# Exponentials of the third to seventh pair one slot later, and another order of the scatters of the first two pairs

## The reference, cut to what matters

```python
z = relu(einsum('bsh,bhk->bsk', x, Wd[ids]) + bd[ids])
y = x + einsum('bsk,bkh->bsh', z, Wu[ids]) + bu[ids]
h = (y - mean(y)) * rsqrt(var(y) + 1e-5) * g[ids] + b[ids]      # 256 wide
p = softmax(h @ gate_w + gate_b)                                # 8 experts
v, i = top_k(p, 2);  v = v / (sum(v) + 1e-9)
mlp = lambda h, e: gelu(h @ w1[e] + b1[e]) @ w2[e] + b2[e]      # 256 -> 1024 -> 256
out = x + h + mlp(h, shared) + sum(v[k] * mlp(h, i[k]) for k in (0, 1))
```

## Time and profile before

| | us |
|---|---|
| median of 3 runs | 625.84 |
| lowest and highest | 624.57, 626.19 |
| the profiled execution's own time | 622.08 |
| its span, first to last instruction | 620.2 |
| TensorE busy in the span | 594.8 (96%) |
| VectorE, ScalarE, GpSimd busy | 501.6, 385.4, 413.3 |
| TensorE's mean granted clock | 0.997 of full speed |

### The profile page before, as it was taken

One profiled execution on the slowest core, in us unless ns is written; L12 is line 12 of the kernel. 1 busy time (PEld: TensorE's weight loads), 2 busy tenths in 40 slices (PEclk: granted clock), 3 DMA queues, 4 the chain that ended last, 5 costly groups with the idle time before them and its releaser, 6 DMA issues.

```text
span 620.2 us, 16942 instructions
## 1 busy us (share of the span) xinstructions
PE 594.8 (96%) x5119; PEld 483.3 (78%) x5119; DVE 501.6 (81%) x1212; ACT 385.4 (62%) x660; POOL 413.3 (67%) x326
## 2 busy tenths in 40 slices
PE   7889979999999999999999999999999999999994
PEld 3556646667566678788888888888888899999883
DVE  4999848879977966898989898989897587887862
ACT  2686928758776845767676767676755455555541
POOL 4564587989885611477868686858697567666682
PEclk9999999999999999999999999999999999999998
DMA  8985656575244945667657656665644335343212
GB/s 285 322 220 150 159 161 183 161 235 115 78 138 153 328 114 171 144 113 149 116 127 133 147 127 127 132 136 128 94 53 72 60 61 66 58 67 64 44 21 32
DMA packets 116740, 81.31 MB, mean 131 GB/s; under 512 B 71090, under 2 KB 106162, under 8 KB 116658
## 3 DMA queue, kind: packets, MB, share of 16 engines
q1 hardware_dynamic: 100802, 60.64, 39.7%
q0 software_dynamic: 13296, 16.92, 15.2%
q10 hardware_dynamic: 2560, 2.69, 1.4%
HBM read 43.21 MB, written 24.42 MB: 109 GB/s over the span
## 4 chain that ended last, share of the span: by engine, by line
PE 68%; DVE 8%; POOL 8%; issue 8%; ACT 4%; DMA 2%; SPq 0%; POOLq 0%; ACTq 0%; DVEq 0%
PE Y L1527 30%; PE H L1501 29%; PE Y L1419 5%; POOL xs_rows L534 3%; PE H L1404 3%; POOL wreg L502 2%; POOL wreg L512 2%; DMA wreg<-in_vecs 1%; ACT hf L685 1%; DVE hl L1160 1%; POOL wreg L516 1%; ACT L685 1%; DVE wreg L808 1%; ACT wreg L623 1%; DVE wreg L949 1%
## 5 line engine op out<-in xcount | busy, mean ns | idle before, releaser
L755 ACT ACTIVATE hf<-H,prme 128x256 f32<-128x256 f32 (+1 forms) x312 | 149.2, 544 | 95.9 <-issue 80.5
L1501 PE MATMUL H<-xT,wreg 128*128 128x256 f16 (+1 forms) x1872 | 194.4, 263 | 0.2
L1527 PE MATMUL Y<-wreg,hh 128*128 x1136 | 188.3, 273 | 0.8 <-DVE hl L1255 0.8
L1501 PEld LDWEIGHTS H<-xT,wreg 128*128 x1872 | 169.0, 98 | 18.9 <-issue 1.0
L1527 PE MATMUL Y<-wreg,hl 128*128 x568 | 154.8, 273 | 0.0
L1527 PEld LDWEIGHTS Y<-wreg,hh 128*128 128x128 f16 x1136 | 111.1, 98 | 15.4 <-issue 1.5
L1255 DVE SCALAR_TENSOR_TENSOR hl<-hf,prme,hh 128x512 f16<-128x512 f32 (+1 forms) x156 | 115.8, 742 | 5.6
L1253 DVE TENSOR_SCALAR hh<-hf,prme 128x512 f16<-128x512 f32 (+1 forms) x156 | 91.1, 584 | 32.5 <-ACT hf L755 30.1
L588 POOL DMA_INDIRECT out_y<-hl,xgm x38 | 69.2, 1820 | 60.6 <-DVE hl L1282 40.9
L577 POOL TENSOR_SCALAR b2w<-b2t,wsel 128x256 f32<-128x256 f32 x71 | 97.9, 1602 | 15.1 <-DVE wsel L1270 9.6
L1404 PE MATMUL H<-xT,wreg 128*128 128x512 f16 x384 | 88.9, 379 | 6.8 <-ACT hf L685 4.7
(11 more groups left out here) (208 smaller groups left out, 663.6 us busy)
## 6 DMA issues: line engine op xcount, KB each, us to landing
stage<-in_w SPq DMA_DIRECT2D x16, 1024.0 KB, 6.2
b2t<-in_b SPq DMA_DIRECT2D x39, 128.0 KB, 3.3
wreg<-in_wpack SPq DMA_DIRECT2D x16, 256.5 KB, 4.7
wreg<-in_xt SPq DMA_DIRECT2D x16, 256.0 KB, 5.3
wreg<-in_vecs SPq DMA_DIRECT2D x16, 256.0 KB, 4.1
out_y<-wreg SPq DMA_DIRECT2D x16, 256.0 KB, 2.8
wreg<-in_x SPq DMA_DIRECT2D x14, 256.0 KB, 5.2
xs_rows<-wreg SPq DMA_DIRECT2D x9, 260.0 KB, 7.1
```

What stands on the lines that cost most here:

```text
L755: act.activation(hf[:, c, half * w:(half + 1) * w], H[c][:, half * w:(half + 1) * w], ACT.Gelu_apprx_tanh, bias=pr[:, ch:ch + 1], scale=pr ...
L1501: m = pe.matmul(H[c][:, half * w:(half + 1) * w], we[:, bass.ds(e + h * 2048 + k * 1024 + col, P)], xp[:, a + k, 0:w], start=i == 0, stop= ...
L1527: m = pe.matmul(result(n, j), hx[:, n % 2, c * w + j * P:c * w + (j + 1) * P], we[:, bass.ds(e + 4096 + h * 2048 + c * D, D)], start=c == ...
```

## The change

It has two parts. On ScalarE, `exps` of pairs 2 to 6 moves from the place of `then(s, 8)` to `then(s, 9)`, a slot later and, within the slot, at the same point. Pairs 0, 1 and 7 keep theirs. On GpSimd, the scatters of pair 0 move from slots 5, 6, 7, 7 to slots 5, 5, 5, 6; of these only groups 0 and 3 stand at the early point of a slot, right behind `root`, and groups 1 and 2 at the slot's end. The scatters of pair 1 keep their slots (8, 9, 10, 10) but move from the early point to the end of each. Nothing is added or taken away, and no wait changes.

```diff
--- before.py
+++ after.py
@@ -88,6 +88,8 @@
 
 def block_slot(p, i):
 
+    if p == 0:
+        return 12 + i // 3
     if p < PT or p == NP - 3:
         return 12 + min(i, 2)
     return 11 + i if p < NP - 2 else 10 + (p < NP - 1) + i // 2
@@ -548,10 +550,9 @@
             for s in range(NS):
                 for p in at(s, 3):
                     root(p)
-                for p in range(PT):
-                    for i in range(4):
-                        if s == base(p) + block_slot(p, i):
-                            scatter(p, i)
+                for i in (0, 3):
+                    if s == base(0) + block_slot(0, i):
+                        scatter(0, i)
                 for p in at(s, 5):
                     rows(2 * p)
                     rows(2 * p + 1)
@@ -563,9 +564,9 @@
                     residual(2 * p)
                     residual(2 * p + 1)
                     tokens(p)
-                for p in range(PT, NP):
+                for p in range(NP):
                     for i in range(4):
-                        if s == base(p) + block_slot(p, i):
+                        if s == base(p) + block_slot(p, i) and (p, i) not in ((0, 0), (0, 3)):
                             scatter(p, i)
 
             def weigh_bias(n):
@@ -714,8 +715,11 @@
                     relu(2 * p)
                 for p in at(s, 1):
                     relu(2 * p + 1)
+                for p in then(s, 9):
+                    if PT <= p < NP - 1:
+                        exps(p)
                 for p in then(s, 8):
-                    if p:
+                    if p in (1, NP - 1):
                         exps(p)
                 for p in at(s, 5):
                     if p >= PT:
```

## The result

The changed kernel takes 619.30 us, the median of four runs (618.67 to 619.6), against 625.21 us for the kernel before: ratio 0.9916, 95% interval 0.9896 to 0.9936. In a second group on the chip the same kernel took 620.33 against 624.04: ratio 0.9937, interval 0.9916 to 0.9959. So the change is worth 3.7 to 5.9 us; the two intervals have 0.9916 to 0.9936 in common, 4.0 to 5.2 us. The forecast was 5.8 us and 620.0.

What follows compares the result with a forecast made beforehand. The prediction took TensorE's 6.5 us of waits, chiefly 3.5 for a GELU behind GpSimd's late `rows`, as the most to win. 4.0 + 2.0 - 0.2 = 5.8 us off 625.84 gave 620.0, range 618.3 to 624.4.

Steps and rivals of the forecast that it cites:

- the sum: First place 4.0, later stalls 2.0, less 0.2 for the transposes: 5.8 us off, 620.0 from the median.
- Which wait ends: GpSimd's `rows` of pair 3 come 8.2 us earlier, ending TensorE's GELU and statistics waits, 4.0 us.
- the hole: GpSimd idle 7.08 us, 64.07 to 71.16, before `root`; four moved scatter DMAs fit there at 5.5 us.
- The 3.5 us for the GELU: TensorE's wait ending at 92.26 us, before matmuls L1404; claimed to go wholly, with 4 us in hand.
- the 0.5 for the statistics: TensorE's wait for L891; claimed to go because the `xb` it needs ends near 79.7 instead of 85.2.
- The transposes: SyncE's four for pair 2 from 66.6 us, now beside four scatters: cost 0.2 us, bounds 0 and 7.4.
- The nearest row: Pair 3's four transposes at 92.9 us, issued right behind scatters: 1268 ns each against a median of 1267.
- the rule that the prediction weighed: VectorE operations with two SBUF inputs and GpSimd operations exclude each other; about 1.5 us of later stalls stand, sum 4.3.
- the stall at 160 us: TensorE's 1.34 us at 160.55, waiting for a tile's last `low_h`; claimed to go with 1.1 us in hand.
- The late stalls: TensorE's 1.34 us at 160.55 and 0.64 at 183.33; both claimed to go, 2.0 us, bounds 0 and 2.0.
- The handover: First routed tile's transpose lands at 223.1, used at 223.37; 0.2 us in hand, cost taken as 0.
- a sign of being wrong: TensorE waiting at the handover to the experts for the first routed tile; no size given.

Runs made afterwards that it cites:

- a_again: The changed kernel once more, no edit: 620.33 us, ratio 0.9937 to the kernel before.
- split_hole: The changed kernel with pair 0's third scatter group behind `root` in slot 6, leaving two DMAs in GpSimd's idle stretch: 622.51 us, ratio 0.9970.
- res_gap: The changed kernel with pair 3's residual adds behind slot 9's scatter, plus pair 0's third scatter group at slot 6's end: 621.08 us, ratio 0.9954.
- res_late: The changed kernel with GpSimd's residual adds of pair 3 behind slot 9's scatter instead of ahead of it: 618.68 us, ratio 0.9907.
- res_all: Against the changed kernel, the residual adds of pairs 3 to 6 stand behind the scatters of their slots: 618.27 us, ratio 0.9907.
- scatter_only: The changed kernel with the exponentials as before, so only the scatters moved: 621.62 us, ratio 0.9954 to the kernel before.
- res_again: The changed kernel with pair 3's residual adds behind slot 9's scatter, measured a second time: 618.73 us, ratio 0.9923.
- b_again: The kernel before once more, no edit: 623.95 us, ratio 0.9995.
- exps_only: The changed kernel with the scatters as before, so only the exponentials moved: 623.51 us, ratio 1.0007 to the kernel before.
- stall_back: The changed kernel plus a TensorE wait before slot 10's second chunk for VectorE's logits of pair 2: 621.81 us, ratio 0.9957.

## Why the prediction was right, and where its sum was off

The time came out as forecast and the main mechanism as described, but the sum did not: TensorE's waits shrank by 3.1 us in the first pair of profiles and not by 5.8. The experts were to start near 217.6; they start at 220.94 and, in a_again, at 220.19, against 223.37 before. So 620.0 was met in part by luck.

**Which wait ends.** Right. The four scatter DMAs ended in the hole at 70.8 (forecast 69.6, and this execution is 0.9 late; the first two were spaced by 2.1 us, more than the 1.6 that the prediction calls the longest and that is a mean), `root` came on time, and `rows` of pair 3 ended at 83.9, 0.9 us of which is the late start, so at 83.0 (forecast 82.2, or 83.5 if `xb` disturbs the gain, which it did). The 3.5 us for the GELU went in every kernel with all of the new scatter order, and 2.4 of it with pair 0's part alone. Of the 0.5 for the statistics, which the sum counts whole, 0.25 stayed in the first profile.

**The transposes, taken at 0.2.** Too small. The nearest row showed that scatters beside them do not slow their issue (1268 ns), and that held: 1276 now. What changed is the landing, median 2.6 to 4.0 us, longest 3.2 to 4.6, of which the argument had a bound and no row for the case. That fewer scatters beside them shorten the wait is supported by split_hole and res_gap, though the median landing there is still 3.8 and 3.7 us. The wait was 0.51, 0.79 and 0.66 in three profiles with none in the hole, 0.55 and 0.66 with two of the DMAs there, and 0.84 to 1.54 in nine with four. The term is 0.6 us rather than 0.2 by the means (1.21 against 0.65).

**What stands behind on VectorE.** This term was missing. I followed the queue of GpSimd and not what its adds do to VectorE when they come earlier: `low_rows` lost 2.9 us and TensorE 1.0 us at `rank`. That the adds hold it is shown by res_late: 4.17 us beside the adds, 1.25 without. It fits the rule that the prediction weighed. By the Trainium skill (SBUF — State Buffer, "SBUF: two separate sides") an add of GpSimd and a VectorE operation with two inputs in SBUF exclude each other. The runs agree with that, but not with the prediction's price of one whole add for each collision: the hold lasted for two adds at `low_rows` and for six in split_hole (8.02 us). The prediction allowed for a collision at the gain (1.3 us, which came) and at the stall at 160 us, where 0.6 to 0.7 us stayed and res_all removes it, and not for one at `low_rows`.

**The late stalls, taken at 2.0.** 1.34 and 0.64 became 0.63 and nothing, with 0.32 new for a transpose of the last pair: 1.0 us net in the first profile. They vary more than I assumed: the second profile of before has 0.28, 0.48 and 0.58 in their place. By the timed pairs the exponentials are worth 1.3 us (621.62 to 620.33) and 1.4 us (620.12 to 618.73) with the new scatter order, and nothing without it. In the profile of the exponentials alone they bring the experts' start forward by 1.36 us, and the wait of 1.34 in the second stage takes that back. Whether the other runs of that kernel lose it in the same way is not shown.

**The handover, taken at 0.** Off by 0.2 in the first profile of the change and by nothing in the second; 0.58, 0.81 and 0.34 in scatter_only, res_again and res_gap, and nothing in the rest. In the first profile the transpose lands 3.2 us after its issue at 217.52, at 220.7, and TensorE starts 0.2 behind it as before: TensorE had come so much earlier that it waits for the landing. The prediction names such a wait as a sign of being wrong; it came, and was small. The wait in the second stage (up to 1.5 us) is in no term of the sum.

**The sum.** By the waits of the first pair of profiles 6.5 - 3.4 = 3.1 us and not 5.8; by the times 3.7 and 5.9. The waits give 0.6 to 2.8 us less than the times. A part of that can be the lower clock behind the stall, which costs 1.5 us where it comes. It was seen in two of three profiles with the stall of 3.50 us (b_again and exps_only, not the first of before), behind the 2.41 in split_hole, and not behind the 3.20 in stall_back: in three of five profiles with a wait of over 2.4 us in this stage, and in none of the nine without one. That speaks for the stall as its cause, but no experiment shows it. The change, which removes the stall, would then gain that too, and no term of the prediction has it. The forecast of 620.0 was hit also because these effects fell on both sides: less won at the waits, and perhaps something at the clock.

## What to carry to other kernels

When a step is moved on one engine, look at which operations of the other engine it will now run beside, and not only at who waits for it: here the adds that came 6.1 us earlier (95.03 to 88.96) cost VectorE 2.9 us at one operation and TensorE 1.0, and placing one scatter ahead of them took that wait away. A row on how fast transfers are issued says nothing of when they land; where a consumer waits for the landing, that is the number to bound. And a stall that ends tells only what is gained there at most: here waits of 5.1 us went (3.5, 1.35 and 0.25), and 2.0 us came back in four others (1.0, 0.5, 0.3 and 0.2), 40% of it. A lead won in one stage must also be followed into the next: in the profile of the exponentials alone 1.36 us were won up to the experts, and a wait of 1.34 behind them took it back.

## What the runs showed of the hardware that was not expected

A VectorE operation on 128 x 4 numbers, 0.17 us alone, was held for 8.02 us through six adds of GpSimd in a row (split_hole), and for 5.47 us through four (res_gap). In the changed kernel three others of that size were held for one add each, in a row of adds as close. Scatter DMAs, issued 0.3 us apart, let VectorE's operation through: 1.25 us beside two of them (res_late). The profile counts the time held as busy: VectorE's busy time is 507.8 us in a_again and 500.9 in b_again, for the same instructions.
